# Banded attention with queries and keys laid out by head in four row groups

## What is computed

```python
x = jnp.transpose(mask, (0, 2, 1))            # n=16, t=256, e=64, H=8, d=8
qkv = x @ w_in.T + b_in
scores = jnp.einsum('bqhd,bkhd->bhqk', q, k) / jnp.sqrt(d)
band = jnp.abs(idx[:, None] - idx[None, :]) <= 64
attn = jax.nn.softmax(jnp.where(band[None, None], scores, neg), axis=-1)
o = jnp.einsum('bhqk,bkhd->bqhd', attn, v).reshape(n, t, e)
o = jnp.transpose(o @ w_out.T + b_out, (0, 2, 1))
y = jax.nn.relu(o) * encodings
out = jnp.einsum('nit,io->not', y, w_ct) + b_ct[None, :, None]
```

## Time and profile before

| | us |
|---|---|
| median of 3 runs | 361.92 (361.88 to 362.2) |
| the profiled execution | 362.1 |
| its span, first to last instruction | 360.4 |

### The profile page before, as it was taken

The page is one execution under the profiler, slowest core; times in us unless marked ns, Lnnn a source line. Parts: engine busy times, 40 slices in busy tenths (PEclk is TensorE's granted clock), DMA queues, the critical chain, the costliest instruction groups (busy, mean ns, idle before and its releaser), DMA issues.

```text
span 360.4 us, 7398 instructions
## 1 busy us (share of the span) xinstructions
PE 320.2 (89%) x2258; PEld 252.3 (70%) x2258; DVE 256.2 (71%) x935; ACT 208.1 (58%) x438; POOL 192.7 (53%) x287
## 2 busy tenths in 40 slices
PE   0689999779798898999999999899999999999993
PEld 0467768567576666767777777777777767888892
DVE  5899999999989899988323615576478846661364
ACT  2639888759687695967841341467577865213210
POOL 4757988758767585856602431515152543244733
PEclk9859999999999999999999999999999999999997
DMA  7996000000000000000000000000000000000011
GB/s 220 363 373 227 1 3 3 1 2 3 1 2 0 3 3 1 3 2 2 2 2 0 0 2 0 1 2 0 2 3 0 2 0 3 0 31 15 1 38 37
DMA packets 10150, 12.16 MB, mean 34 GB/s; under 512 B 1920, under 2 KB 8832, under 8 KB 10112
## 3 DMA queue, kind: packets, MB, share of 16 engines
q1 hardware_dynamic: 9536, 11.36, 9.2%
q10 hardware_dynamic: 576, 0.33, 0.4%
HBM read 10.64 MB, written 1.05 MB: 32 GB/s over the span
## 4 chain that ended last, share of the span: by engine, by line
PE 58%; DVE 27%; issue 8%; ACT 3%; POOL 2%; DMA 1%; POOLq 0%; DVEq 0%; SPq 0%; ACTq 0%
DVE masked L1110 10%; PE S L666 6%; PE S L339 5%; PE O L377 4%; PE ST L690 4%; PE S L472 4%; PE ST L361 4%; PE S L608 2%; PE S L536 2%; PE PJ L449 2%; PE PJ L579 2%; PE O L623 2%; PE PJ L310 2%; DVE st L1072 2%; PE XB L597 2%
## 5 line engine op out<-in xcount | busy, mean ns | idle before, releaser
L1110 DVE CUSTOM_DVE_ANT_0 masked<-S,band 128x192 bf16<-128x192 f32 x256 | 79.1, 353 | 8.4 <-PE S L339 7.3
L785 ACT ACTIVATE ex<-ST 128x384 f32<-128x384 f32 x128 | 62.2, 489 | 14.0 <-PE ST L361 13.4
L339 PE MATMUL S<-qk 128*128 128x384 f32 x128 | 53.5, 424 | 10.2 <-DVE mw L1110 8.1
L948 POOL TENSOR_SCALAR rstd<-mv 128x1 f32<-128x1 f32 x40 | 11.8, 294 | 94.2 <-DVE mv L1074 94.0
L960 POOL TENSOR_TENSOR qk<-kp,kmask 128x1024 fp32r<-128x1024 f32 x24 | 46.3, 1934 | 5.0 <-DVE kp L1208 4.9
L361 PE MATMUL ST<-qk 128*128 128x192 f32 x256 | 48.7, 273 | 0.0
L361 PEld LDWEIGHTS ST<-qk 128*128 128x128 f32 x256 | 44.5, 189 | 1.9 <-issue 1.2
L339 PEld LDWEIGHTS S<-qk 128*128 128x128 f32 x128 | 24.8, 195 | 23.3 <-issue 16.1
L1254 DVE TENSOR_REDUCE mw<-S 128x8 f32<-128x512 f32 x32 | 22.0, 687 | 17.9 <-PE S L536 17.8
L751 ACT ACTIVATE hs<-PJ,sb,cols 128x512 fp32r<-128x512 f32 x29 | 22.5, 777 | 20.6 <-PE PJ L311 20.1
L377 PE MATMUL O<-ex,v 128*32 128x192 f32 x512 | 34.2, 338 | 0.0
(11 more groups left out here) (178 smaller groups left out, 757.9 us busy)
## 6 DMA issues: line engine op xcount, KB each, us to landing
w<-in_w SPq DMA_DIRECT2D x2, 1024.0 KB, 10.1
cx<-in_cx SPq DMA_DIRECT2D x1, 1024.0 KB, 7.9
cxT<-in_cxT SPq DMA_DIRECT2D x1, 1024.0 KB, 9.6
up<-in_up SPq DMA_DIRECT2D x1, 1024.0 KB, 10.9
down<-in_down SPq DMA_DIRECT2D x1, 1024.0 KB, 11.8
out<-x SPq DMA_DIRECT2D x8, 128.0 KB, 1.7
x<-in_x SPq DMA_DIRECT2D x1, 768.0 KB, 5.6
vecs<-in_vecs SPq DMA_DIRECT2D x1, 640.0 KB, 8.0
```

Of the source, the lines that this page charges most:

```text
L339: mm(out, r32(qp[:, t % 2, g, b, P * c:P * c + P]), r32(mv_), start=True, stop=True).then_inc(s["pe_s"], 1)
L785: A(ex[:, (n // 2) % 4, 2 * w:2 * w + 2, :], ST[n % 2][:, 0:2 * WIN].rearrange("p (h k) -> p h k", h=2), ACT.Exp, scale=SCALE).then_inc(s[ ...
L1110: last = V.tensor_tensor_reduce(out=masked[:, n % 2, h, :], in0=S[n % 2][:, WIN * h:WIN * h + WIN], in1=band[:, c, :], scale=1.0, scalar=N ...
```

## The change

The partitions of q and k are now ordered (j, r, d): head j has the 32 partitions 32j to 32j+31, 24 of them for the three copies and one, 32j+24, for the maximum. A unit is (b, g, j), one head with both query halves c. S of a unit is two matmuls (c = 0, 1) of 192 columns, with 32 partitions as contraction, and so is ST. The masked copies `kb`, their buffer, `keys`, `KB` and `KA` are gone; `kp` has three buffers.

The maxima go to a small tile `top`; GpSimd negates them into a zeroed `neg` (slot lag 9), and TensorE forms q with the maxima in place by adding them in PSUM (lag 10): the identity times q, 512 columns, then four small matmuls of `neg` with the identity. ScalarE copies all 128 rows into a buffer of their own, `qm`, which ST reads. ST comes 13 slots after S instead of 11. The selects run once for four units (four instructions at a time); PV runs in odd slots, c = 0 at lag 16 and c = 1 at lag 18 from the fourth unit, and `ex` has three buffers of four units. O is copied at lag 26 (was 24), and what follows moves by two slots, the choice of rows by one or two.

At the start, weights are brought into the new order by a GpSimd copy `w0p`; `b0` and the new `colp` come by eight small transfers on ScalarE's queue, ahead of `kmask` and `wv0`, and VectorE waits for all eight before `w0h`. `mw` of the later attention now lies in `cx` and is cleared after the slots.

```diff
-ST_LAG, PV_LAG = 11, 16
+NEG_LAG, MT_LAG, ST_LAG, PV_LAG, O_LAG = 9, 10, 13, (16, 18), 26
...
-                    mv_ = kb[:, t % 2, g, 2 * w:2 * w + 2, b, BAND * c:BAND * c + WIN]
-                    out = S[n % 2][:, 0:2 * WIN].rearrange("p (h k) -> p h k", h=2)
-                    mm(out, r32(qp[:, t % 2, g, b, P * c:P * c + P]), r32(mv_), start=True, stop=True).then_inc(s["pe_s"], 1)
...
+                    for c in range(2):
+                        last = mm(S[n % 2][:, WIN * c:WIN * c + WIN], r32(qp[rows(j), t % 2, g, b, P * c:P * c + P]),
+                                  r32(kp[rows(j), t % 3, g, b, BAND * c:BAND * c + WIN]), start=True, stop=True)
+                    last.then_inc(s["pe_s"], 1)
...
+                    for c in range(2):
+                        last = mm(ST[n % 2][:, WIN * c:WIN * c + WIN], r32(kp[rows(j), t % 3, g, b, P * c:P * c + P]),
+                                  r32(qm[rows(j), t % 2, g, b, BAND * c:BAND * c + WIN]), start=True, stop=True)
...
+                t, r = place(T_, l, MT_LAG)
+                if r % 8 == 0 and live(t, r):
...
+                    mm(MT[:, :].rearrange("p (g q) -> p g q", g=2), r32(identr[:, :]), r32(qp[:, t % 2, :, b, :]), start=True, stop=False)
+                    for g in range(2):
+                        for c in range(2):
+                            last = mm(MT[:, T * g + P * c:T * g + P * c + P], r32(neg[:, b, 2 * c + g, :]), r32(identr[:, :]),
+                                      start=False, stop=(g, c) == (1, 1))
...
+                for c in range(2):
+                    t, r = place(T_, l, PV_LAG[c])
+                    if r % 4 == 3 and live(t, r):
...
+                        for j in range(4):
+                            last = mm(O[rows(j), T * g + BAND * c:T * g + BAND * c + WIN],
+                                      v0[:, t % 2, c, b, 4 * g + j, :], ex[:, q % 3, j, c, :],
+                                      start=(c == 0), stop=(c == 1), skip_group_check=True)
...
-            load(b0[:, :], a["b0"], "ld_w0")
+            for j in range(4):
+                load(b0[rows(j), :], a["b0"].rearrange("(r j d) n -> j r d n", r=4, j=4)[j], "ld_b0")
+                load(colp[rows(j), :], a["cols"].rearrange("(r j d) n -> j r d n", r=4, j=4)[j][:, :, 0:2], "ld_b0")
...
-                        last = A(r32(kb[:, t % 2, 1, j, 1, :]), kp[:, 1, 1, :], ACT.Copy, scale=kmask[:, j:j + 1])
...
-                    A(r32(qp[96:128, t % 2, :, r // 8, :].rearrange("p g (c q) -> p c g q", c=2)),
-                      MT[96:128, :].rearrange("p (c g q) -> p c g q", c=2, g=2), ACT.Copy, scale=-1.0)\
...
+                    A(r32(qm[:, t % 2, :, b, :]), MT[:, :].rearrange("p (g q) -> p g q", g=2), ACT.Copy).then_inc(s["act_mt"], 1)
...
+            G.tensor_copy(w0p, w0[:, :, :].rearrange("p n (r j d) -> p n j r d", r=4, j=4)).then_inc(s["pool_w0"], 1)
...
-                G.tensor_tensor(r32(kb[:, t % 2, g, :, b, :]), kp[:, g, b:b + 1, :].to_broadcast([P, 4, T]),
-                                kmask[:, :, None].to_broadcast([P, 4, T]), ALU.mult).then_inc(s["pool_kb"], 1)
...
+                    G.tensor_scalar(r32(neg[:, b, :, :].rearrange("p a (j f) -> p a j f", f=32)[:, :, :, 24]), top[:, b, :, :], -1.0, None, ALU.mult)\
+                        .then_inc(s["pool_neg"], 1)
...
-            dve.wait_ge(s["ld_w0"], 32)
-            V.tensor_copy(r32(w0h[:, :, :]), w0[:, :, :]).then_inc(s["dve_w"], 1)
+            dve.wait_ge(s["ld_b0"], 16 * 8)
+            dve.wait_ge(s["pool_w0"], 1)
+            V.tensor_copy(r32(w0h[:, :, :]), w0p).then_inc(s["dve_w"], 1)
```

More of the change, by code:

```diff
@@ L120, in build @@
         hT = sb("hT", [P, FC, 512])
+        w0p = hT[:, 4:8, 0:P]
         xT = sb("xT", [P, 2, N * E])
@@ L164, in parts, with rows @@
         def parts(r):
-            return r // 8, (r % 8) // 4, (r % 4) // 2, r % 2
+            return r // 8, (r % 8) // 4, r % 4
+        def rows(j):
+            return slice(32 * j, 32 * j + 32)
         def xg(t, k):
@@ L327, in slot_ @@
                     n = UNITS * t + r
[L328 to L332, removed]
+                    b, g, j = parts(r)
                     if r in (0, 4):
@@ L363, in slot_ @@
                     last.then_inc(s["pe_st"], 1)
[L366 to L380, removed]
@@ L381, in slot_ @@
-                t, r = place(T_, l, 26)
-                if l % 8 == 2 and live(t, r):
+                t, r = place(T_, l, MT_LAG)
+                if r % 8 == 0 and live(t, r):
+                    b = r // 8
+                    k = 2 * t + b
+                    pe.wait_ge(s["pool_neg"], k + 1)
+                    if k == 0:
+                        pe.wait_ge(s["dve_ident"], 1)
+                    if k >= 1:
+                        pe.wait_ge(s["act_mt"], k)
+                    if b == 0 and T_ >= 3:
+                        pe.wait_ge(s["fa_x"], T_ - 2)
+                    mm(MT[:, :].rearrange("p (g q) -> p g q", g=2), r32(identr[:, :]), r32(qp[:, t % 2, :, b, :]), start=True, stop=False)
[3 more added lines that the diff above has]
+                                      start=False, stop=(g, c) == (1, 1))
+                    last.then_inc(s["pe_mt"], 1)
@@ L383, in slot_ @@
+                t, r = place(T_, l, O_LAG + 2)
+                if r % 8 == 0 and live(t, r):
                     k = 2 * t + r // 8
@@ L406, in slot_ @@
                 t = T_ - 3
-                if l == 2 and 0 <= t < TILES:
+                if l == 4 and 0 <= t < TILES:
                     pe.wait_ge(s["f_sc"], t + 1)
@@ L750, in slot_ @@
                             act.wait_ge(s["dve_mix"], m - 1)
-                        A(r32(hs[:, m % 2, :]), proj_bank(t, n)[:, :], ACT.Identity, bias=sb0[:, n:n + 1], scale=cols[:, n // 2:n // 2 + 1])\
+                        A(r32(hs[:, m % 2, :]), proj_bank(t, n)[:, :], ACT.Identity, bias=sb0[:, n:n + 1], scale=colp[:, n // 2:n // 2 + 1])\
                             .then_inc(s["act_hs"], 1)
[L753 to L760, removed]
-                        last = A(r32(kb[:, t % 2, 1, j, 1, :]), kp[:, 1, 1, :], ACT.Copy, scale=kmask[:, j:j + 1])
-                        if j == 3:
-                            last.then_inc(s["act_kb"], 1)
                 if l == 0 and 0 <= T_ < TILES:
@@ L987, in slot_ @@
-                t = T_ + 1
-                if l in KB and 0 <= t < TILES:
-                    keys(t, *KB[l])
+                t, r = place(T_, l, NEG_LAG)
+                if r % 8 == 0 and live(t, r):
+                    b = r // 8
+                    k = 2 * t + b
+                    pool.wait_ge(s["dve_max"], 8 * k + 8)
+                    if k >= 2:
+                        pool.wait_ge(s["pe_mt"], k - 1)
+                    else:
+                        pool.wait_ge(s["pool_zero"], 3)
+                    G.tensor_scalar(r32(neg[:, b, :, :].rearrange("p a (j f) -> p a j f", f=32)[:, :, :, 24]), top[:, b, :, :], -1.0, None, ALU.mult)\
+                        .then_inc(s["pool_neg"], 1)
```

185 lines of the change are left out of this document (88 added, 97 removed).

## The result

The changed kernel takes 452.38 us (451.24 to 452.73, 4 runs) against 362.06 us (361.88 to 362.44, 4 runs) before: ratio 1.249, interval 1.246 to 1.251. The forecast was 367.4 with a range up to 374, slower the likelier sign. The sign was right; of the 90 us, 5 were foreseen.

A forecast was written before the change was run, and what follows sets the result against it. VectorE bounds full tiles by little, with TensorE close behind and taking its place. Start +2.0, tile 0 -1.7, tile 1 +1.4, tiles 2 to 6 +0.5, tile 7 +1.2, end +2.0: sum +5.4, forecast 367.4 us; range 353.5 to 374.

The forecast's parts named there:

- What bounds the kernel now: Tiles 2 to 6 (21.2 us): VectorE 19.9 plus 1.2 us of gap, TensorE 19.8 with waits; VectorE ahead by little.
- VectorE's relief, -1.9 us a tile: Without key copies beside them, VectorE steps such as cmp and sel shorten: 18.0 us a tile instead of 19.9.
- Tile 0, -1.7, and tile 1, +1.4: Tile 0 loses about 1.7 us of VectorE stretching; tile 1, bound by TensorE, gains 1.9 less 0.5 of idle.
- S and ST side by side, -1.3: Row groups overlap: ST starts while the second half of S runs, 0.08 us a slot, 1.3 us a tile.
- A change of shape, 0.19 us each: TensorE switching between full array and 32-row S and ST costs 0.19 us each, 2.7 us a tile.
- count of 14 changes: Added shape changes in a tile's 16 slots: 9 going back to S plus 5 entered from ST.
- +0.5 us for the maxima: One 512-column matmul and four small ones replace four transposes on TensorE: +0.23 us, twice a tile.
- TensorE per tile: +1.9: TensorE's sum per tile: +2.7 for shape changes, +0.5 for maxima, -1.3 for overlap.
- the rival without overlap: Shape changes paid, but S and ST do not overlap: +1.3 us in tiles 1 to 7, 376.4 us; chance 12%.
- TensorE takes the place of VectorE: Tiles 2 to 6: TensorE 21.3 us against VectorE's 19.2, so +0.1 us a tile, +0.5 for five.
- Start, +2.0: Eight small loads on ScalarE's queue delay VectorE's w0h: +2.9 us (2.3 to 3.5), less 0.9 at L1077.
- Tile 7 +1.2 and the end +2.0: Tile 7 has 3 shape changes fewer: +1.2 us; the end has two uncovered slots, 1.1, and drain changes, 0.9.

The follow-up runs named there:

- all rows: Changed kernel with S and ST reading all 128 partitions instead of the 32 of their head (another output): 367.8 us.
- two loads: b0 and colp laid out ahead and brought by two loads instead of eight: with S and ST on all 128 partitions 360.25 us; in the changed kernel 445.8 us.
- 64-row kernel: Changed kernel with S on partitions 0 to 63 and ST on 64 to 127 (another output): 378.0 us.
- The strips: Kernel with S and ST on all 128 rows, plus one idle matmul onto a strip of 32 columns ahead of S in each slot: 371.1 us.

## Why the prediction was wrong, step by step

*What bounds the kernel now:* right as read; cutting the copies gained 7.0 us without touching TensorE, as VectorE's share in the earlier trace rows said.

*VectorE's relief, -1.9 us a tile:* right: it is busy for 18.1 us in a full tile on average instead of 19.9. Beside no key copy `cmp` takes 421 ns and `sel` 346 in the changed kernel, about their least lengths in the earlier trace rows.

*Tile 0, -1.7, and tile 1, +1.4:* neither came. With all rows they took 16.0 and 17.0 us, as before. In tile 0 VectorE's busy time did fall, from 15.2 to 13.8 us, but not the tile's length. The clock in it was lower (0.57 against 0.68), but with two loads, at 0.68 again, it still took 15.7 us. The all-row kernel has no changes of shape around S and ST, so its tile 1 says nothing of their price.

*S and ST side by side, -1.3:* the mechanism is right (0.01 us apart), the size too small. I had ST start beside the second half of S, 0.08 us a slot; but the first halves start together too, and S and ST in pairs follow every 0.11 us at the full clock (second view below), 0.22 us for a slot's four matmuls, where with all rows S alone takes 0.20 (103.66 to 103.86 in that trace). Where no change of shape comes between, that is some 0.2 us a slot, an estimate from these rows. What I didn't see is that it also bears on the clock: 378 against 476 us at 64 rows.

*A change of shape, 0.19 us each:* about right at the full clock. In the 64-row kernel a full-array step is followed by S after 0.21 us instead of 0.12, and S by its second half after 0.19 instead of 0.09 (0.11 in this kernel where no change goes before, see the second view):

```profile
111.58 0.28 PE L318 MATMUL PJ<-xs,w0l 128*128 128x256 f32 x1
111.79 0.35 PE L341 MATMUL S<-qk 64*128 64x192 f32 x1
111.80 0.35 PE L354 MATMUL ST<-qk 64*128 64x192 f32 x1
111.99 0.27 PE L341 MATMUL S<-qk 64*128 64x192 f32 x1
```

```profile
113.98 0.27 PE L341 MATMUL S<-qk 64*128 64x192 f32 x1
114.09 0.27 PE L341 MATMUL S<-qk 64*128 64x192 f32 x1
114.20 0.27 PE L341 MATMUL S<-qk 64*128 64x192 f32 x1
```

That a change of tiling mode drains the engine (the Trainium skill, TensorEngine Tiling (Array Packing), Key Properties) agrees with the first view in its 0.09 us added at the first S. The 0.08 to 0.10 at the second half, which has the same shape, fits a weight load that is no longer hidden, as I had put it in the prediction; no run takes the two apart. Too high is what I made of it for a tile: I put 21.3 us and with the full clock it is 20.3 (64 rows) against 20.0 (all rows). Part of this is TensorE's waits, which I had carried over in full. In tiles 3 to 5 of the 64-row kernel the wait for `sel` (3.3 us in the earlier trace rows) is gone and that for `on` is 1.7 us instead of 2.2; others came, 1.3 us for GpSimd's selects, 1.1 for `yr` and 1.0 for the exponentials. Neither the count of 14 changes nor the +0.5 us for the maxima was measured by itself.

*The clock:* the failed step, and nearly the whole miss. "TensorE per tile: +1.9" takes durations from the earlier trace rows, all at clock 1.00, and nowhere asks whether the clock stays there when S and ST use a quarter of the rows. A tile went from 21.2 to 31.3 us on average instead of 21.3. No rival had it: the rival without overlap, the range's upper end and "TensorE takes the place of VectorE" all assumed the full clock. The clock column of the earlier trace rows was in front of me and only read as "1.00".

*Start, +2.0:* too small by 3.8 us. The step that failed is the issue time taken from one plain load (0.45 us; it was 0.64) and the landing (3.4 to 4.6 us after the last issue; it was 5.9). The sum was also wrong in itself: 7.8 to 9.0 against 4.6 is 3.2 to 4.4 later, not 2.3 to 3.5; it seems that the 0.9 us of L1077 was taken off inside the range and once more behind it. With two loads the first reduction comes at 14.5 us, so the rest of the step, that the start gains from the missing key copies, is right: 0.6 us earlier than before.

*Tile 7 +1.2 and the end +2.0:* at the full clock, with all rows, tile 7 took 17.1 us (+1.8), and the end 193.6 instead of 191.2 us (+2.4). Near, as far as these kernels stand for it; in the changed one the low clock makes them +10.6 and +11.7.

What stays open: a version of the change itself (32 rows, right output) at the full clock was not found, so what it would take there is known only from the 64-row kernel. That kernel is at 378.0 with 6.9 us lost in tile 1 (23.9 against 17.0 in the earlier trace rows, at clock 0.54) and a first reduction 5.6 us later than before (20.7 against 15.1 us); 378.0 - 6.9 - 5.6 and the 2.0 that I had put for the start give 367.5, an estimate for the forecast's own case. That it meets the forecast of 367.4 is luck and confirms nothing. In the 64-row kernel tiles 2 to 6 took 4.5 us less than before, where I had put 0.5 more; tile 0 took 18.4 us, where I had put 14.3; the part after the last tile took 3.6 us more than before, where I had put 2.0; and the 6.9 us assume that tile 1 would take exactly its old time. Open too is how rows and changes of shape add up where the clock is undecided between its levels (each of these kernels ran once, and a second run could fall otherwise): 65 rows without changes (421.2) against 64 rows on one half with them (476.0), and ST alone on all rows (515.5) above 32 rows in both (452.4), are differences that how many rows are at work does not give by itself. The strips show that changes alone, with all rows in use, leave the clock at full; they do not show that they count for nothing where fewer rows are.

## What to carry to other kernels

Before cutting a matmul's contraction rows, ask what the clock will do: TensorE can be busy all the time and fall to half its clock because most of its rows are not at work, and then every other matmul of the stage pays. If small-row matmuls are wanted, place them so that different row groups run at once, and look at the clock row first: two halves of 64 rows at once held the full clock here, two groups of 32 did not. A long GpSimd instruction on plain SBUF data can hold VectorE for its whole length; cutting it in pieces cost GpSimd about a third more time for these copies and gave 7.0 us (1.9%), more than any version of the large change.

## What the runs showed of the hardware that I had not expected

- The clock depends on the rows at work, not on TensorE's busy time alone. The same S and ST: all rows 367.8 us; 64 rows side by side 378.0; 65 rows one after the other 421.2; 32 rows side by side 452.4; 64 rows one after the other 476.0; S on 32 and ST on 128, one after the other, 515.5. These times hold the clock, the overlap and the changes of shape together.
- With 65 rows the clock goes back and forth in a steady stream of the same work, with tiles of 20.6 and 28.9 us next to each other in one run. Whether a low clock keeps itself low is not shown.
- The clock record can be wrong: 1.0 (0.999 on average) in a run whose weight loads took 306 ns instead of 194.
- Running side by side pays more at the lower level: 37.9 against 31.5 us a tile (an estimate of 6 us from two kernels that also differ in rows).
- Issuing a load whose rows are taken from a rearranged source costs 0.64 us, once 1.22, against 0.45 for a plain one, though it moves a quarter of the bytes or less.
